# A seven-product second layer in the third part of a one-core FFN, attention, FFN kernel

## The reference

```python
x = x + 0.5 * _L0_ffn_ref(_layernorm(x, axis=-1), ...)
x = x + _L0_attn_ref(_layernorm(x, axis=-1), ...)
x = x + 0.5 * _L0_ffn_ref(_layernorm(x, axis=-1), ...)

def _L0_ffn_ref(x, k0, k1, k2, s0, s1, s2):
    h = jnp.concatenate([x, -x], axis=-1)
    h = s0 * _conn_dense(k0, h)
    h = jax.nn.relu(h) * 2
    h = s1 * _conn_dense(k1, h)
    h = jax.nn.relu(h) * 2
    h = s2 * _conn_dense(k2, h)
    return h
```

## Time and profile before

| | us |
|---|---|
| median of 3 runs | 1561.07 (1561.02 to 1564.03) |
| the profiled execution | 1562.64 |
| its span | 1560.9 |
| first layer of chunk 0 of the third part, without a gap, would start at | 1199.90 |
| one chunk of the third part | 45.03 |

### The profile page before, as it was taken

How to read it: one execution, slowest core, us unless ns; L and a number is a source line. 1 busy time by engine, 2 the same in 40 slices (tenths; PEclk the granted TensorE clock), 3 DMA queues, 4 the chain that set the end, 5 groups by cost and what they waited for, 6 DMA issues and landing times.

```text
span 1560.9 us, 35447 instructions
## 1 busy us (share of the span) xinstructions
PE 1536.5 (98%) x14112; PEld 724.2 (46%) x14112; DVE 1119.5 (72%) x1616; ACT 841.1 (54%) x1703; POOL 193.6 (12%) x516
## 2 busy tenths in 40 slices
PE   6999999999999999999999999999999999999998
PEld 3555555555443334333333334434333555555554
DVE  6535543564668998999989999989896667666552
ACT  3223322322167888888888888888886222222221
POOL 4300000000111122121112121112220000000000
PEclk9999999999999999999999999999999999999999
DMA  5121023202041222211222211222220222211210
GB/s 172 28 68 54 13 67 91 71 13 67 2 123 48 70 70 63 69 36 50 63 70 63 83 44 61 71 83 63 70 71 27 81 68 72 75 51 56 81 27 14
DMA packets 146227, 96.39 MB, mean 62 GB/s; under 512 B 106544, under 2 KB 125616, under 8 KB 146096
## 3 DMA queue, kind: packets, MB, share of 16 engines
q1 hardware_dynamic: 146096, 94.54, 21.0%
HBM read 49.15 MB, written 37.75 MB: 56 GB/s over the span
## 4 chain that ended last, share of the span: by engine, by line
PE 95%; SPq 2%; DMA 1%; DVE 1%; ACT 1%; issue 0%
PE ffn_mm L437 28%; PE ffn_mm L1311 17%; PE ffn_mm L1331 16%; PE ffn_mm L423 7%; PE ffn_acc L453 7%; PE ffn_acc L659 6%; PE ffn_tr L659 5%; PE ffn_mm L754 4%; PE ffn_acc L568 2%; PE ffn_acc L766 2%; SPq L313 1%; DMA k_u<-L_ffn_k 1%; PE ffn_tr L407 1%; PE ffn_tr L665 1%; DVE m_part L680 1%; SPq L314 0%
## 5 line engine op out<-in xcount | busy, mean ns | idle before, releaser
L1287 ACT ACTIVATE probs<-ffn_mm 128x512 f32<-128x512 f32 (+1 forms) x960 | 471.2, 557 | 88.0 <-PE ffn_mm L1311 83.0
L680 DVE TENSOR_REDUCE m_part<-ffn_acc 128x2 f32<-128x1024 f32 (+1 forms) x348 | 369.9, 1063 | 34.1 <-PE ffn_acc L659 27.4
L1311 PE MATMUL ffn_mm<-qk 128*32 128x512 f16 (+7 forms) x5120 | 386.5, 353 | 3.4 <-ACT probs L1287 2.1
L437 PE MATMUL ffn_mm<-ffn_h1h,w 128*128 128x512 f16 x1024 | 388.3, 379 | 0.0
L437 PE MATMUL ffn_mm<-ffn_h1l,w 128*128 128x512 f16 x1024 | 388.1, 379 | 0.0
L680 DVE TENSOR_REDUCE m_part<-ffn_tr 128x2 f32<-128x1024 f32 (+2 forms) x292 | 308.4, 1056 | 40.1 <-PE ffn_tr L659 26.2
L1331 PE MATMUL ffn_mm<-probs,v 128*32 128x512 f32 (+3 forms) x1920 | 236.5, 551 | 0.0
L503 ACT ACTIVATE ffn_h2h<-ffn_mm 128x512 f16<-128x512 f32 x128 | 76.4, 597 | 296.2 <-PE ffn_mm L437 294.7
L1311 PEld LDWEIGHTS ffn_mm<-qk 66*32 66x32 f16 (+1 forms) x5120 | 135.0, 94 | 208.5 <-ACT probs L1287 91.0
L514 DVE SCALAR_TENSOR_TENSOR ffn_h2l<-ffn_mm,ffn_h2h 128x512 f16<-128x512 f32 x128 | 85.7, 686 | 166.8 <-ACT ffn_h2h L503 166.8
L437 PEld LDWEIGHTS ffn_mm<-ffn_h1h,w 128*128 128x128 f16 x1024 | 100.1, 98 | 118.9 <-issue 1.8
(11 more groups left out here) (123 smaller groups left out, 1196.8 us busy)
## 6 DMA issues: line engine op xcount, KB each, us to landing
qk<-qk_scr SPq DMA_DIRECT2D x256, 64.0 KB, 2.7
ctx_scr<-ctx_out SPq DMA_DIRECT2D x64, 256.0 KB, 2.6
qk<-ctx_scr SPq DMA_DIRECT2D x56, 256.0 KB
v_scr<-v_pad SPq DMA_DIRECT2D x32, 256.0 KB, 3.7
v<-v_scr SPq DMA_DIRECT2D x16, 512.0 KB, 4.1
x_res<-L_attn_x SPq DMA_DIRECT2D x8, 512.0 KB, 3.8
qk_scr<-qk_hi SPq DMA_DIRECT2D x32, 128.0 KB, 1.9
qk_scr<-qk_lo SPq DMA_DIRECT2D x32, 128.0 KB, 1.9
```

The lines of the kernel that those rows point to most:

```text
L437: ins = nc.tensor.matmul(f.mm[:, m % 4, :], w1[:, kt, m * P:(m + 1) * P], part[:, kt, :], start=(kt == 0 and part is f.h1h), stop=(kt == H ...
L680: nc.vector.tensor_reduce(m_part[u][:, t, :, r], s_ps[slot][:, :, 0:w], AX.X, ALU.max).then_inc(sb.s_done, 1)
L1287: nc.scalar.activation(prob_tile(g, j, slice(c0, CH)), st_ps[bank(k)][:, c0:CH], ACT.Exp, scale=scale_now).then_inc(se.exp_done, 1)
L1311: ins = nc.tensor.matmul(st_ps[bank(k)][c:c + 32, c0:CH], k_part(pair % 2, h, rows, slice(kb * P + c, kb * P + c + 32)), q_part(pair % 2, ...
```

## The change

The 1024 x 1024 product of the second layer is cut into quarters: 512 x 512 of the weights against 512 hidden rows x 256 tokens. Eight products of quarters would do it; seven do, if sums and differences of quarters are multiplied (the scheme of Winograd and Strassen). The four differences of weights (`pool_diff`, eight POOL operations) are made once, in the second part, one per head pair, at step `FIRST_SUM_STEP` of pairs 1 to 8, into the first part's `h2h` and `h2l`.

In each chunk of the third part:

- ACT copies the first layer with `relu` to fp32 (`h32`), not to fp16.
- POOL makes four sums of quarters, S1 to S4 (`hidden_sums`, 1024 elements each), from all of `h32`.
- For the seven operands A11, A12, S1, S2, S3, S4, A22 ACT writes a fp16 high part (`high`) and DVE a low part (`low`), 1024 elements each. DVE's reads two SBUF operands.
- TensorE does p1, (output projection of the next chunk), p2, p5, p6, p7, p3, p4. Each is 32 matmuls of 256 columns, in two halves, each half in a bank of its own out of a ring of six (four of `mm`, two of `tr`). Then come the first layer of the next chunk (`pe_first_layer`) and the third layer of this one (`third_layer`).
- ACT copies p1 and p5 out. DVE adds the others to what lies in SBUF (`add`: c11, u2, u3, c12, c21), POOL does u4 and c22 (`sbuf_sums`, four operations of 512 elements). ACT and DVE split c11, c22, c12, c21 into `h2h` and `h2l` (`out_high`, `out_low`).
- POOL takes over the two additions of the normalisation (`context_sums`), and DVE's reciprocal is cut in four (`inverse`), one of them ahead of the u2 additions and three behind c21. The normalisation for chunk c + 2 is done in chunk c.

The banks of the next first layer are free when DVE has read them: tiles 0 and 1 wait for u3, 2 and 3 for c12, 4 and 5 for c21, 6 and 7 for ACT's first copies of the new chunk. The core of the diff:

```diff
+        DIFFS = ((d1, w1_12, w1_11), (d3, w1_22, w1_12), (d2, w1_22, d1), (d4, w1_21, d2))
+        def pool_diff(n):
...
+            nc.gpsimd.tensor_tensor(dst[:, rows, :], a[:, rows, :], b[:, rows, :], ALU.subtract).then_inc(sq.diff, 1)
...
+            BANK_READ = {"p6": sq.s1, "p7": sq.c11, "p3": sq.s5, "p4": sq.u2}
...
+            @block.gpsimd
...
+                def chunk(c, more_ctx=True):
+                    hidden_sums(c)
+                    if more_ctx:
+                        context_sums(c + 2)
+                    sbuf_sums(c)
...
+                def sbuf_sums(c):
+
+                    for n in range(2):
+                        wait(pool, sq.u2, c * 2 + n + 1)
+                        wait(pool, sq.s5, c * 2 + n + 1)
+                        nc.gpsimd.tensor_tensor(one[:, n, :], two[:, n, :], five[:, n, :], ALU.add).then_inc(sq.u4, 1)
+                    for n in range(2):
+                        wait(pool, sq.u3, c * 2 + n + 1)
+                        nc.gpsimd.tensor_tensor(five[:, n, :], three[:, n, :], five[:, n, :], ALU.add).then_inc(sq.c22, 1)
...
             @block.vector
...
+                def chunk(c, last=False, more_ctx=True):
+                    low(c, (S1, S2))
                     if not last:
                         add_attention(c + 1)
+                    low(c, (S3,))
+                    for n in range(2):
+                        add(c, n, three, one, sq.s1, "p2", sq.c11)
                     if not last:
                         dve_x_rows(f, ln3, c + 1)
+                    for n in range(2):
+                        out_low(c, "c11", n)
+                    low(c, (S4, A22))
+                    if more_ctx:
+                        inverse(c + 2, range(0, 1))
+                    for n in range(2):
+                        add(c, n, two, one, sq.s1, "p6", sq.u2)
+                    for n in range(2):
+                        add(c, n, three, two, sq.u2, "p7", sq.u3)
+                    for n in range(2):
+                        out_low(c, "c22", n)
+                    for n in range(2):
+                        add(c, n, one, one, sq.u4, "p3", sq.c12)
+                        out_low(c, "c12", n)
+                    for n in range(2):
+                        add(c, n, two, three, sq.u3, "p4", sq.c21)
+                        out_low(c, "c21", n)
+                    if more_ctx:
+                        inverse(c + 2, range(1, 4))
+                        normalize(c + 2)
+                    if not last:
+                        low(c + 1, (A11, A12))
                     dve_residual(f, c)
...
             @block.scalar
...
                 def chunk(c, last=False):
+                    for n in range(2):
+                        copy(one, n, "p1", sq.s1, c)
+                    high(c, (S2, S3))
                     if not last:
                         act_ln_sqrt(ln3, c + 1)
+                    high(c, (S4,))
+                    for n in range(2):
+                        out_high(c, "c11", n)
                     if not last:
                         act_x_rows(f, ln3, c + 1)
+                    high(c, (A22,))
+                    for n in range(2):
+                        copy(five, n, "p5", sq.s5, c)
+                    for name in ("c22", "c12", "c21"):
+                        for n in range(2):
+                            out_high(c, name, n)
                     if not last:
+                        hidden(c + 1, range(0, HALF))
+                        high(c + 1, (A11,))
+                        hidden(c + 1, range(HALF, HT))
+                        high(c + 1, (A12, S1))
...
             @block.tensor
...
+                    second_layer(c, None if last else project)
                     if not last:
+                        pe_first_layer(c + 1, layer_free(c + 1), range(HT))
+                    third_layer(c, lambda j: wait(pe, f.sem.res, c * 2 + j - 1) if last else wait(pe, se.x2, c * 2 + j + 3))
```

More of the change, by code:

```diff
@@ L197, in __init__ @@
         self.bo_add = new("bo_add")
+class QuarterSems:
+    def __init__(self, new):
+        self.h32 = new("h32")
+        self.sum = new("sum")
+        self.hi = new("hi")
+        self.lo = new("lo")
+        self.p1 = new("p1")
+        self.p5 = new("p5")
+        self.p6 = new("p6")
+        self.p7 = new("p7")
+        self.p2 = new("p2")
+        self.p3 = new("p3")
+        self.p4 = new("p4")
+        self.s1 = new("s1")
+        self.s5 = new("s5")
+        self.u2 = new("u2")
+        self.u3 = new("u3")
+        self.u4 = new("u4")
+        self.c11 = new("c11")
+        self.c12 = new("c12")
+        self.c21 = new("c21")
+        self.c22 = new("c22")
+        self.out_hi = new("out_hi")
+        self.out_lo = new("out_lo")
+        self.diff = new("diff")
+        self.gate = new("gate")
 class PhaseCSems:
@@ new lines, in quarter_of @@
+            def quarter_of(k, t):
+                return h32[:, k * HALF:(k + 1) * HALF, T_HALF[t]]
+            sum1 = v_buf[1][:, :, :].rearrange("p t e -> p (t e)").rearrange("p (m n) -> p m n", m=HALF)
+            source = {A11: quarter_of(0, 0), A12: quarter_of(1, 0), A22: quarter_of(1, 1),
+                      S1: sum1, S2: ln2.xn[:, :, :], S3: ln1.xn[:, :, :], S4: quarter_of(0, 1)}
+            room = qk_buf[1][:, :, :].bitcast(F32).rearrange("p q (s n) -> p q s n", s=2)
+            one, five, two, three = (room[:, q, :, :] for q in range(4))
@@ new lines, in build, with out_place, pair_of, out_count @@
+            OUT_KT = {"c11": (0, 0), "c22": (HALF, 1), "c12": (HALF, 0), "c21": (0, 1)}
+            OUT_ORDER = ("c11", "c22", "c12", "c21")
+            OUT_FROM = {"c11": three, "c22": five, "c12": one, "c21": two}
+            def out_place(buf, name, n):
+                kt, t = OUT_KT[name]
+                return buf[:, kt + 2 * n:kt + 2 * n + 2, T_HALF[t]]
+            def pair_of(view):
+                return view.rearrange("p (m n) -> p m n", m=2)
+            def out_count(c, name, n):
+                return c * 8 + 2 * OUT_ORDER.index(name) + n + 1
@@ L1371, in _ @@
+            PARTS = tuple((kt, slice(hf * D, (hf + 1) * D)) for kt in range(DT) for hf in range(2))
             @block.sync
@@ L1424, in _ @@
                 dve_x(f, 0)
[L1425 to L1430, removed]
+                inverse(1, range(0, 3))
+                low(0, (A11, A12))
+                inverse(1, range(3, 4))
+                normalize(1)
+                for sem in (sb.ctx_st0, sb.ctx_st1):
+                    dve.wait_ge(sem, 8 * BATCH * PAIRS * QCH)
@@ new lines, in high, with copy @@
+                def high(c, ops):
+                    for x in ops:
+                        if x in (A11, A12, A22):
+                            wait(act, sq.h32, c * HT + (HALF if x == A11 else HT))
+                        else:
+                            wait(act, sq.sum, c * 4 + (S1, S2, S3, S4).index(x) + 1)
+                        nc.scalar.activation(hi_op[x], source[x], ACT.Copy).then_inc(sq.hi, 1)
+                def copy(dst, n, product, done, c):
+                    wait(act, READY[product], c * 2 + n + 1)
+                    nc.scalar.activation(dst[:, n, :], product_bank(product, n), ACT.Copy).then_inc(done, 1)
@@ new lines, in out_high @@
+                def out_high(c, name, n):
+                    ready = {"c11": sq.c11, "c22": sq.c22, "c12": sq.c12, "c21": sq.c21}[name]
+                    if name == "c11" and n == 0:
+                        wait(act, f.sem.l2_ps, c * 2)
+                    wait(act, ready, c * 2 + n + 1)
+                    src = pair_of(OUT_FROM[name][:, n, :])
+                    nc.scalar.activation(out_place(h2h, name, n), src, ACT.Relu).then_inc(sq.out_hi, 1)
+                hidden(0, range(0, HALF))
@@ L1498, in _ @@
+                pe.wait_ge(sq.diff, 2 * len(DIFFS))
+                pe_first_layer(0, layer_free(0), range(1, HT))
                 chunk(0, first=True)
```

196 lines of the change are left out of this document (155 added, 41 removed).

## The result

The changed kernel takes 1620.84 us (1620.10 to 1622.21), the kernel before 1561.69 in the same comparison: a ratio of 1.0386, 95% interval 1.0372 to 1.0400. That is 59.1 us more; 49.7 were forecast.

What follows compares the result with a forecast made beforehand. TensorE, busy 98% of the span, bounds the kernel. Third part: 7.7 + 57 + 261.5 + 46.5 + 34.6 = 407.3 against 357.6, 49.7 more: 1612.3 us profiled, 1611 as a median; range 1564 to 1624.

Steps and rivals of the forecast that it cites:

- TensorE's gain: Third part: seven products make TensorE's chunk 42.07 us, 2.96 less, 23.7 us over eight chunks if nothing else ends later.
- The ladder: Third part: output additions queued behind low parts waiting for ACT delay the next first layer; 46.6 us a chunk without contention.
- The kind of hold: Third part: a DVE operation with two SBUF operands waits for POOL's whole running operation, 2.37 us each.
- turn-taking: Third part: DVE and POOL alternate, each waiting a whole operation of the other; 53.4 us a chunk, +58 everywhere.
- VectorE first: Third part: DVE keeps its place with several two-operand SBUF operations in a row; 51.1 us a chunk, +40.
- +24: Third part: short holds, DVE waiting for POOL no longer than in the earlier rows (0.6 us); 48.3 us a chunk.
- The context sums' place: Third part: context load lands 13 us after its issue at about -2.5; layer norm waits 1.9 for the context sum.
- Second part: Eight weight differences on POOL, one per pair, cost nothing where POOL idles; without that cover 19 us.
- (a): Rival, third part: POOL's lock on DVE costs nothing, only the queued additions hold; +9.8, 1571 us; chance 0.13.
- (b): Rival, third part: queued additions over 4.5 us shorter than laid out, TensorE stays the bound; 1539 us; chance 0.12.
- (c): Rival: TensorE's clock falls from 2.4 GHz in longer pauses; part of the products at 1.2 GHz, over 1624; chance 0.05.

Runs made afterwards that it cites:

- both edits together: Changed kernel with DVE's c12 and c21 additions ahead of the output low parts, and POOL's hidden and context sums cut to 2 columns: 1540.15 us, ratio 0.9868.
- the run that takes the holds away: Changed kernel with POOL's four hidden and two context sums per chunk cut to 2 columns, every wait kept: 1574.0 us, ratio 1.0089.
- the run with a clock of 1.00: Changed kernel with TensorE also running unread products where it would stand still, ahead of p1 and p3 and in the first layer: 1623.2 us, ratio 1.0402.

## Why the prediction was right, and where it was short

The starts of p1 in the changed kernel are 1205.92, 1263.34, 1319.02, 1374.42, 1429.05, 1481.56, 1536.26 and 1582.25; the last residual ends at 1616.24. Against the sum:

| Stretch | forecast, us | measured, us |
|---|---|---|
| to the first p1 (from 1199.90, as before) | 7.7 | 6.0 |
| to the second p1 | 57 | 57.4 |
| five chunks | 261.5 | 272.9 |
| the one without context sums | 46.5 | 46.0 |
| the last, to its residual | 34.6 | 34.0 |
| the third part | 407.3 | 416.3 |
| more than the 357.6 before | 49.7 | 58.7 |

- **TensorE's gain**: right. 109 ns a matmul, and 41.6 to 41.7 a chunk where nothing holds it (both edits together).
- **The ladder**: right. 46.8 measured without holds against 46.6; rungs of 1.98 against 1.96; VectorE's stall at c22 2.71 against 2.6; POOL on 512 elements 1.27 against the 1.25 drawn between 0.69 and 2.37.
- **The kind of hold**: right. Normalisation 2.6, A11 and A12 3.4 each in place of 1.2. Whole operations of 2.4 us hold, not 0.7 at a time.
- **The step that was short** is the choice of 52.3 a chunk, "between" turn-taking (53.4) and VectorE first (51.1). The trace shows turn-taking wherever both have such operations in a row: in the row at 1315.52 each of the two low parts waits for one of POOL's sums, and POOL's next sum for the low part. Five chunks of 53.4 in place of 52.3 make the sum 55.2 more. The prediction gives +58 for turn-taking, and in the same way +40 and +24, where the other chunks of its sum unchanged give 43.7 and 29.7; it shows no working for the difference, so that 58 lies close to the measured 59.1 is in part luck. The earlier trace rows had it: there each of VectorE's two operations ends with one POOL operation, and the next begins beside the next. No row of before spoke for VectorE first, so the middle had no evidence of its own.
- **What is left**: the measured chunk is 54.6 (272.9 / 5 by the starts of p1; the five range from 52.5 to 55.7), 1.2 over 53.4. By the starts of the layer norm, mean of five, it is 54.4, that without context sums 50.8, that without either 46.9: the hidden sums cost 3.9, where 3.3 + 1.7 (a later p1, a later addition) was written, the context sums 3.6 where 1.9 was. One group was charged 1.1 too much and the other 1.7 too little: that these nearly cancel is luck. The context sums' place was wrong too: I had the load land about 10.5 behind p1, beside the layer norm. SyncE issues it behind the store of an earlier chunk, which waits for the residual, so POOL starts at 1337.61, 18.6 behind p1, beside the low parts of x and c11 (3.40 and 3.42 for operations of 1.22 and 1.28). Moving the load gave at most 2.3 us back: two POOL sums hold two operations of VectorE in either place.
- **Second part**: right, the differences cost nothing.
- **Rivals**: (a), ladder without holds, 1571: the run that takes the holds away gave 1574.0. (b), TensorE the bound, 1539: the run with both taken away gave 1540.2. (c): the clock did fall, to 0.91 over a chunk, which I gave 0.05; but the run with a clock of 1.00 gave nothing back. "Part of the products at 1.2 GHz would take it over 1624" was wrong in its consequence: the slow products lie almost all where TensorE waits, and cost some 2 us in all.

## What to carry to other kernels

An engine that is idle is not free: before work goes to POOL, list what VectorE does at that time with two SBUF operands, and charge each a whole POOL operation, taking turns; here four hidden sums cost 3.9 us a chunk and two context sums 3.6. Put the operations that free the busiest engine's banks in front of those that only use its results: here that took 40 us off with the same work (1620.8 to 1580.5), and a further 29 us went when VectorE's reciprocals, residual and projection additions were spread among its low parts, beside POOL's sums (to 1551.8). Of the versions with all the work only the one with both is faster than the kernel before.

## What the runs showed of the hardware that was not expected

- POOL and VectorE alternate when both have a row of such operations: POOL's sums last 3.2 to 3.4 us in place of 2.36, VectorE's low parts 3.36 in place of 1.22.
- Tiny operations are held as large ones are: 0.16 us became 1.82 in the layer norm. One with a single tensor operand was held as well (TENSOR_SCALAR on 128x4 fp32, 1.41 for 0.17; the earlier trace rows has one of 0.65). The reciprocals (1.72), the batch statistics and all that read PSUM were not.
- A POOL fill of 1024 fp32 elements takes 0.95 us and holds nothing.
- TensorE's clock was at its lower level in three stretches of a chunk (0.52, 0.56, 0.50), behind waits for VectorE of 2.5 and up to 4.5 us and behind a row of short ones of about 1 us; behind a pause of 2.1 us, at 1374.42, it was 1.00. This cost some 2 us of 59, as VectorE set the pace.
